# Batch 0's rows of the last expert picked by matmuls from SBUF, its other rows gathered while that expert runs

## The reference, cut to what matters

```python
probs = softmax(xr @ Wg); gate_vals, expert_idx = top_k(probs, 2)
# every row has a slot in each of its two experts; an expert holds C = 640 rows, later rows are dropped
dispatched = xr[dispatch_mask.reshape(-1) % S].reshape(E, C, d)       # 8 x 640 x 256
h = relu(einsum('ecd,edf->ecf', dispatched, w1))                      # 256 -> 1024
expert_out = einsum('ecf,efd->ecd', h, w2)                            # 1024 -> 256
out = gate_0 * (row of the first choice) + gate_1 * (row of the second choice)
```

## Time and profile before

| | us |
|---|---|
| median of three runs | 990.11 |
| the profiled execution | 992.42 |
| its span (first to last instruction) | 990.7 |
| PE busy | 916.7 (93%) |
| DVE busy | 605.8 (61%) |
| ACT busy | 492.0 (50%) |
| POOL busy | 439.3 (44%) |

### The profile page before, as it was taken

One profiled execution on the slowest core, in us unless ns is written; L12 is line 12 of the kernel. 1 busy time (PEld: TensorE's weight loads), 2 busy tenths in 40 slices (PEclk: granted clock), 3 DMA queues, 4 the chain that ended last, 5 costly groups with the idle time before them and its releaser, 6 DMA issues. The chain is left out here.

```text
span 990.7 us, 16978 instructions
## 1 busy us (share of the span) xinstructions
PE 916.7 (93%) x5620; PEld 718.8 (73%) x5620; DVE 605.8 (61%) x1961; ACT 492.0 (50%) x887; POOL 439.3 (44%) x416
## 2 busy tenths in 40 slices
PE   6899999999899999999992889999999779999997
PEld 4566766765688999999982556576756468888886
DVE  5677798988763444444444687887786246363535
ACT  6366666665333344443336265767676344343332
POOL 4453444436742333232236455455263455535333
PEclk9799999999999999999995898999999699999999
DMA  5443222201225322323104663534320010212201
GB/s 186 159 177 112 97 75 97 75 20 41 102 99 190 136 86 96 138 103 130 69 21 139 222 223 96 177 113 159 123 75 23 1 54 1 97 45 74 81 39 42
DMA packets 51964, 98.88 MB, mean 100 GB/s; under 512 B 7579, under 2 KB 23835, under 8 KB 51766
## 3 DMA queue, kind: packets, MB, share of 16 engines
q1 hardware_dynamic: 48822, 89.62, 26.3%
q0 software_dynamic: 3072, 8.39, 2.7%
HBM read 61.63 MB, written 36.36 MB: 99 GB/s over the span
## 5 line engine op out<-in xcount | busy, mean ns | idle before, releaser
L906 ACT ACTIVATE a_probs<-a_ps_b 128x512 f32<-128x512 f32 x240 | 142.0, 602 | 65.3 <-PE a_ps_b L985 62.4
L540 POOL TENSOR_SCALAR_AFFINE_SELECT a_probs<-a_probs 128x512 f32<-128x512 f32 x128 | 80.8, 649 | 136.2 <-ACT a_probs L906 136.1
L2074 PE MATMUL exp_ps_o<-w_both,exp_h_hi 128*128 128x512 f32 x320 | 115.7, 402 | 0.7 <-POOL w_both L1960 0.7
L985 PE MATMUL a_ps_b<-a_q_st,a_k_st 104*128 104x256 f32 (+3 forms) x384 | 104.7, 335 | 2.9 <-ACT a_probs L906 2.1
L1987 ACT ACTIVATE exp_h_hi<-shared 128x320 fp32r<-128x320 f32 x128 | 54.3, 440 | 86.0 <-PE shared L2057 86.0
L1274 DVE CUSTOM_DVE_ANT_0 a_masked_s<-shared,a_mask_f 128x512 f32<-128x512 f32 (+1 forms) x128 | 76.6, 620 | 31.8 <-PE shared L966 29.5
L2220 POOL TENSOR_TENSOR dense_h_lo<-dense_mixed,dense_h_hi 128x512 fp32r<-128x512 f32 x40 | 53.2, 1330 | 96.6 <-ACT dense_h_hi L2285 96.6
L1274 DVE CUSTOM_DVE_ANT_0 a_masked_s<-a_ps_a,a_mask_f 128x512 f32<-128x512 f32 (+1 forms) x128 | 76.5, 621 | 31.6 <-PE a_ps_a L966 29.0
L966 PE MATMUL a_ps_a<-a_k_st,a_q_st 96*128 96x512 f32 (+1 forms) x192 | 89.7, 483 | 5.8 <-DVE a_nmax L1274 5.0
L2031 DVE SCALAR_TENSOR_TENSOR exp_h_lo<-shared,exp_h_hi 128x320 fp32r<-128x320 f32 x128 | 61.4, 490 | 54.6 <-ACT exp_h_hi L1987 53.8
L966 PE MATMUL shared<-a_k_st,a_q_st 96*128 96x512 f32 (+1 forms) x176 | 90.0, 519 | 3.1 <-DMA a_k_st<-scratch 3.1
(11 more groups left out here) (326 smaller groups left out, 2244.8 us busy)
## 6 DMA issues: line engine op xcount, KB each, us to landing
w_raw<-in_m_w SPq DMA_DIRECT2D x16, 1024.0 KB, 5.4
scratch<-a_hi SPq DMA_DIRECT2D x24, 512.0 KB, 3.0
dense_mix_rows<-mix_rows SPq DMA_DIRECT2D x9, 768.0 KB, 6.4
scratch<-a_lo SPq DMA_DIRECT2D x24, 256.0 KB, 3.2
a_q_st<-scratch SPq DMA_DIRECT2D x64, 96.0 KB, 2.2
a_k_st<-scratch SPq DMA_DIRECT2D x64, 96.0 KB, 2.3
exp_rows<-dispatched SPq DMA_DIRECT2D x9, 640.0 KB, 3.9
dispatched<-kept_sub SPq DMA_DIRECT2D x9, 512.0 KB, 2.8
```

The source lines that it names most:

```text
L540: nc.gpsimd.affine_select(out=blocks, in_=blocks, compare_op=ALU.is_ge, fill=0.0, base=0, pattern=[[0, HPG], [1, P]], channel_multiplier=- ...
L906: nc.scalar.activation(probs[:, k, :], ps_b[k % B_BANKS][:, :], ACT.Exp, scale=scale).then_inc(exps, 1)
L985: last = nc.tensor.matmul(ps[:, at:at + wd], k_st[t % STACKS][0:TAIL, h, j * P:(j + 1) * P], q_st[t % STACKS][0:TAIL, h // PER_TILE, j * P ...
L2074: nc.tensor.matmul(bank[:, :], h[0][:, f, rows_at], w2["both"][:, f, :, :].rearrange("p k d -> p (k d)"), start=(f == 0), stop=False, skip ...
```

## The change

Three things, in the words of the code:

- **Expert 7's rows of batch 0 are selected on chip.** DVE writes `last_slots` (for each row of batch 0 the greater of its two slots) and `last_gate` (the weight with which the row uses expert 7, or 0) after batch 0's routing. SP writes the slots to a small DRAM tensor and, in the expert phase, reads them back to all partitions (`slot_rows`). In the second expert of every turn of the expert loop DVE writes five one-hot matrices `slot_hot` (128x512 each), one after every third half block; those of the last turn are used. When expert 7's output tiles are in `out`, ACT splits off the high part of each (`last_hi`), POOL the low part of the first four and DVE that of the last one, and PE multiplies: 5 tiles x 4 tiles of rows x 2 parts = 40 matmuls of 256 columns, placed after the loop, into the shared PSUM banks. DVE adds the result times `last_gate` to `sub`.
- **The other rows of batch 0 are gathered inside expert 7.** POOL's loop is cut to three turns and its last turn written out, without the split of a further w1. After the last w2 split POOL waits until expert 6 is stored and issues the eight gathers of batch 0 into `sub`. ACT and DVE weigh and add them. The rows of `results` that belong to expert 7 are zeroed beforehand by two more clearing transfers in attention 0. In attention 1 batch 0 begins with the statistics; POOL issues one gather of tile 4 ahead of the first root and three gathers (tile 4's other and tile 5's two) between the roots. ACT clears the second and third key stack later, after the first projections; DVE's `small_constants` stands after the first variance. SP stores expert 7's rows only once the gathers have landed.
- **PE's order at the end of attention 0.** `first_of_chip(2, 0)` and `(2, 1)` stand behind the projection of batch 3, `(2, 2)` behind its router transposes; `(2, 3)` stays at the end. Of the `keep_busy` ahead of `rt` one is left of three, ahead of `lg` none, and at the start of the expert phase one of two.

```diff
@@ attention_phase, SP @@
-                if rope and T < 6:
-                    clear_slots(3 * T, 3 * T + 3)
+                if rope and T < 7:
+                    clear_slots(3 * T, min(3 * T + 3, 2 * (E0 + 2)))
...
+                sp.wait_ge(first["slots_in"], 1)
+                sp.dma_start(first["list"], first["slots"][:, :]).then_inc(first["slots_out"], 16)
@@ attention_phase, POOL (layer 1) @@
-                for n in range(TPB + 1):
-                    gather(n)
+                gather(TPB, (0,))
                 combine_root(0, 0)
+                gather(TPB, (1,))
                 gather(TPB + 1)
                 combine_root(1, 0)
@@ attention_phase, ACT (layer 1) @@
                 clear_values(2 * TPB + 1)
-                for i in range(1, STACKS):
-                    clear_stack(i)
...
                 for j in ORDER[2:4]:
                     upper_evac(0, j)
+                for i in range(1, STACKS):
+                    clear_stack(i)
@@ attention_phase, PE (layer 0) @@
-            FINAL_TURNS = {("ot", BATCH - 1, 0): 1, ("rk", 2, 0): 1, ("rt", BATCH - 1, 0): 3, ("lg", BATCH - 1, 0): 1}
+            FINAL_TURNS = {("ot", BATCH - 1, 0): 1, ("rk", 2, 0): 1, ("rt", BATCH - 1, 0): 1}
...
                     first_of_memory()
-                    first_of_chip(2, 0)
                 fill_whole(name)
+                if rope and name == ("out", BATCH - 1, 1):
+                    for i in range(2):
+                        first_of_chip(2, i)
+                if rope and name == ("rt", BATCH - 1, 1):
+                    first_of_chip(2, 2)
             if rope:
-                for i in range(1, TPB):
-                    first_of_chip(2, i)
+                first_of_chip(2, TPB - 1)
@@ attention_phase, DVE @@
+            def last_expert_of_first():
+                at = slice(0, TPB)
+                nc.vector.tensor_tensor(first["slots"][:, :], slot[:, 0, at], slot[:, 1, at], ALU.max).then_inc(first["slots_in"], 1)
+                for k in range(2):
+                    last = nc.vector.scalar_tensor_tensor(last_gate[:, k, :], slot[:, k, at], float((E0 - 1) * CAP),
+                                                          gates[:, k, at], ALU.is_ge, ALU.mult)
+                after(last)
+                after(nc.vector.tensor_tensor(first["gate"][:, :], last_gate[:, 0, :], last_gate[:, 1, :], ALU.add))
...
-                small_constants()
-                for i in range(TPB):
-                    combine_sum(0, i)
-                combine_variance(0, 0)
+                for i in range(TPB):
+                    nc.vector.bn_stats(c_stats[:, i, :], tile(sub, i)).then_inc(c_stats_done[0], 1)
+                combine_variance(0, 0)
+                dve.sem_inc(scaled_done, TPB)
+                dve.sem_inc(summed, TPB)
+                small_constants()
...
+                    if rope and (T, s) == (16, 3):
+                        last_expert_of_first()
@@ expert_phase, SP @@
             load_weights(sp, "w1", w1, w1_in, 1)
+            sp.wait_ge(first["slots_out"], 16)
+            sp.dma_start(slot_rows[:, :], first["list"].rearrange("p n -> (p n)").unsqueeze(0).to_broadcast([P, SEQ]))\
+              .then_inc(slot_rows_in, 16)
...
             store(sp, E0 // PAIR - 1, 0)
+            sp.wait_ge(near_rows, 16 * 2 * TPB)
@@ expert_phase, POOL @@
-            with pool.Fori(0, E0 // PAIR) as it:
+            with pool.Fori(0, E0 // PAIR - 1) as it:
...
+            lower(w2, w2_hi_ready, E0 - 1, w2_ready)
+            lower(w1, w1_hi_ready, E0 - 1, w1_ready)
+            lower(w2, w2_hi_ready, E0, w2_ready)
+            pool.wait_ge(stored[0], 16 * (E0 // PAIR + 1))
+            pool.wait_ge(stored[1], 16 * (E0 // PAIR))
+            pool.wait_ge(first["scattered"], 16 * 2 * TILES)
+            for n in range(TPB):
+                for k in range(2):
+                    nc.gpsimd.indirect_dma_start(
+                        out=sub[:, k * TPB + n, :], out_offset=None, in_=results[:, :],
+                        in_offset=bass.IndirectOffsetOnAxis(ap=get_at[:, k, n:n + 1], axis=0),
+                        bounds_check=SLOTS - 1, oob_is_err=False).then_inc(near_rows, 16)
+            for t in range(CT - 1):
+                pool.wait_ge(last_hi, t + 1)
+                nc.gpsimd.tensor_tensor(last_part(1, t), out[PAIR - 1][:, t * D:(t + 1) * D], last_part(0, t).bitcast(F32),
+                                        ALU.subtract).then_inc(last_lo, 1)
@@ expert_phase, ACT, after its loop @@
+            act.wait_ge(t_free, E0 * T_FILLS + T_FILLS + T_BANKS)
+            for t in range(CT):
+                act.wait_ge(o_free, (E0 - 1) * O_FILLS + t + 1 + O_BANKS)
+                nc.scalar.copy(last_part(0, t), out[PAIR - 1][:, t * D:(t + 1) * D]).then_inc(last_hi, 1)
+                if t == 0:
+                    act.wait_ge(near_rows, 16 * 2 * TPB)
+                    for n in range(TPB):
+                        nc.scalar.activation(sub[:, n, :], sub[:, n, :], ACT.Identity, scale=gates[:, 0, n:n + 1])\
+                            .then_inc(near_scaled, 1)
@@ expert_phase, DVE @@
+                        if p == 1 and n % 3 == 0 and n // 3 < CT:
...
+                            nc.vector.tensor_scalar(slot_hot[:, n // 3, :].rearrange("q (i p) -> q i p", i=TPB),
+                                                    slot_rows[:, :].rearrange("q (p i) -> q i p", i=TPB), slot_ids[:, n // 3:n // 3 + 1], None,
+                                                    ALU.is_equal).then_inc(hots_done, 1)
...
+            dve.wait_ge(last_hi, CT)
+            nc.vector.tensor_tensor(last_part(1, CT - 1), out[PAIR - 1][:, (CT - 1) * D:CT * D],
+                                    last_part(0, CT - 1).bitcast(F32), ALU.subtract).then_inc(end_lo, 1)
+            for n in range(TPB):
+                dve.wait_ge(near_scaled, n + 1)
+                nc.vector.scalar_tensor_tensor(sub[:, n, :], sub[:, TPB + n, :], gates[:, 1, n:n + 1], sub[:, n, :], ALU.mult,
+                                               ALU.add).then_inc(near_sums, 1)
+            dve.wait_ge(near_sums, TPB)
+            for n in range(TPB):
+                dve.wait_ge(picked_full, n + 1)
+                nc.vector.scalar_tensor_tensor(sub[:, n, :], picked(n), first["gate"][:, n:n + 1], sub[:, n, :], ALU.mult,
+                                               ALU.add).then_inc(near_done, 1)
@@ expert_phase, PE @@
-            keep_busy(nc, ps_o[0], ident, keep["x"][:, 0:2, :].rearrange("p a d -> p (a d)"), 2)
+            keep_busy(nc, ps_o[0], ident, keep["x"][:, 0:2, :].rearrange("p a d -> p (a d)"), 1)
... after the loop
+            pe.wait_ge(u_free, E0 * U_FILLS + U_BANKS)
+            pe.wait_ge(hots_done, CT * (E0 // PAIR))
+            for t in range(CT):
+                pe.wait_ge(last_hi, t + 1)
+                if t < CT - 1:
+                    pe.wait_ge(last_lo, t + 1)
+                else:
+                    pe.wait_ge(end_lo, 1)
+                for i in range(TPB):
+                    for k in range(2):
+                        last = nc.tensor.matmul(picked(i), slot_hot[:, t, i * P:(i + 1) * P], last_part(k, t),
+                                                start=(t == 0 and k == 0), stop=(t == CT - 1 and k == 1),
+                                                skip_group_check=True)
+                    if t == CT - 1:
+                        last.then_inc(picked_full, 1)
```

More of the change, by code:

```diff
@@ L484, in clear_slots @@
                     e, at = divmod(m, 2)
-                    slots = w["dispatched"][e * CAP:(e + 1) * CAP, :].rearrange("(p t) d -> p t d", t=CT)
+                    rows = w["dispatched"][e * CAP:(e + 1) * CAP, :] if e <= E0 else w["results"][(E0 - 1) * CAP:E0 * CAP, :]
+                    slots = rows.rearrange("(p t) d -> p t d", t=CT)
                     a, n = at * CLEAR, min(CLEAR, CT - at * CLEAR)
@@ L530, in normalise @@
                 if b == BATCH - 1 and i == 0 and rope:
-                    pool.wait_ge(keep["cleared"], 16 * (E0 + 1) * -(-CT // CLEAR))
+                    pool.wait_ge(keep["cleared"], 16 * (E0 + 2) * -(-CT // CLEAR))
                 nc.gpsimd.tensor_scalar(tile(sub, n), tile(x, n), mean[:, n:n + 1],
@@ L621, in rows_lower, with gather @@
                                         ALU.subtract).then_inc(rows_lo, 1)
-            def gather(n):
+            def gather(n, choices=(0, 1)):
                 if n >= DEEP:
                     pool.wait_ge(summed, n - DEEP + 1)
-                for k in range(2):
+                for k in choices:
                     nc.gpsimd.indirect_dma_start(
@@ L1113, in first_of_memory @@
                                                  w1["rows"][:, t, c * P:(c + 1) * P], ident[:, a - t * P:z - t * P],
-                                                 start=(a == half * HALF), stop=False, skip_group_check=True)
+                                                 start=False, stop=False, skip_group_check=True)
```

(24 more changed lines are left out.)

13 lines of the change are left out of this document (9 added, 4 removed).

## The result

The changed kernel takes 1005.66 us (median of 4 runs, 1004.17 to 1007.25); the kernel before, run beside it, 990.23 (4 runs). The ratio is 1.0167, 95% interval 1.0144 to 1.0191. The prediction was 982.4 us: the time moved the other way. The profiled execution after took 1004.17 us (span 1002.4), 11.75 more than that of before (992.42, span 990.7).

A forecast was written before the change was run, and what follows sets the result against it. It took the end of the experts to be set by the chain from last output tile through store and gathers to batch 0's rows; 3.9 - 12.7 + 0.4 - 1.0 + 1.7 = -7.7 against 990.11 gave 982.4 us, range 978.8 to 986.5.

The forecast's parts named there:

- 1c: Inside the experts: expert 7's gathers are hidden and the five selections of each odd expert fit DVE's idle time; cost 0.
- The rival on the slower side: Odd experts' hidden layers: DVE becomes the bound, and from about 1.85 us a selection the gain is lost; chance 0.05.
- The rival of strided reads: Odd experts: each selection takes 1.1 us, twice 0.55, through its step of four; +1.4 us, 983.8; chance 0.15.
- 1a: Tail of the experts: 40 selection products take 5.0 us, then DVE's additions, so layer 1 starts later; +3.9 us.
- 1b: Head of layer 1: batch 0's gathers, waits and sums go, rows come earlier; -12.7 us, net -8.8 with 1a.
- Selection bound by weight loads: Tail of the experts: the 40 products take 7.3 us in place of 5.0; +2.3 us, 984.7; chance 0.10.
- the +0.4: Head of layer 1: PE's turns, waiting for weights, end after the rows; shorter transposes give half back; +0.4 us.
- Late gathers in expert 7: POOL let go only at 512 instead of 502, so rows land at 525; +3.5 us, 985.9; chance 0.05.
- Part 2: End of attention 0: with PE's new order the rank products come earlier and PE ends at 278.7; -1.0 us.
- the clock: Start of the experts: PE stands still longer, its clock falls, 3.4 us at half speed; +1.7 us, bounds 0 and 3.4.

The follow-up runs named there:

- two_turns_again: Rerun on the third chip of `two_turns`, beside `all_moved_again`: two turns in place of one at the experts' start; 975.37 us, ratio 0.9854.
- all_moved: The changed kernel with the five selections of odd experts behind half blocks 0, 2, 4, 5 and 13, none where POOL splits w2; 979.71 us, ratio 0.9894.
- two_turns: `all_moved` with two turns in place of one at the experts' start, on a slower chip; 997.27 us, ratio 0.9945.
- old_order: `all_moved` with PE's old order at the end of attention 0 and both turns at the experts' start, on a slower chip; 997.49 us, ratio 0.9943.
- old_order_again: Rerun of `old_order` on the third chip, beside `all_moved_again`; 979.22 us, ratio 0.9891.
- probe_reduce: The kernel before with one DVE tensor_reduce on SBUF added behind half block 6 of each odd expert, third chip; 987.75 us, ratio 0.9973.
- all_moved_again: Rerun of `all_moved`, the same kernel, on the third chip; 979.94 us, ratio 0.9893.
- third_moved: The changed kernel with only the third selection of odd experts moved, from behind half block 6 to behind 5; 984.75 us, ratio 0.9949.
- narrow: The changed kernel with only 32 of the third selection's 512 values behind half block 6, the other 480 behind 13; 999.56 us, ratio 1.0082.
- contiguous: The changed kernel with selections reading and writing in plain order, without the step of four (another result, same work); 1004.01 us, ratio 1.0121.
- probe_scalar: The kernel before with one contiguous 512-value DVE tensor_scalar on SBUF added behind half block 6 of odd experts, slower chip; 1024.5 us, ratio 1.0217.

## Why the prediction was wrong, step by step

**1c, the selections: the step that failed.** It counted DVE's idle time, 0.39 in each half block and 1.17 in three, and put the cost at 0. The rate was near: 0.68 each against 0.55 assumed, well inside 1.17. What it left out is that the third lands in POOL's split of w2 and is held until the end of it. That costs 3.8 us of PE's waiting and 2.7 more that go with the half clock behind it, 6.5 an odd expert, 26 in all. The rival on the slower side, with a chance of 0.05, named the right engine, experts and wait, but as a rate of 1.85 us or more a piece; no selection but the held one is slower than 0.7, and one instruction does it all. The rival of strided reads is refuted too: a step of four gives 0.68, not 1.1, and no loss (the experts take 234.5 us in `two_turns_again`, with the strided selections, and 234.6 before).

The trace of before did show it, in rows that I didn't read. First DVE, then POOL, in the kernel before, in layer 1's attention:

```profile
591.21 1.29 DVE L1510 SCALAR_TENSOR_TENSOR kept_x<-kept_sub,a_c_inv,kept_x 128x256 f32<-128x256 f32 x1
592.42 0.54 DVE L1274 CUSTOM_DVE_ANT_0 a_masked_s<-a_ps_a,a_mask_f 128x384 f32<-128x384 f32 x1
...
592.89 1.29 DVE L1510 SCALAR_TENSOR_TENSOR kept_x<-kept_sub,a_c_inv,kept_x 128x256 f32<-128x256 f32 x1
```
```profile
590.67 1.54 POOL L707 TENSOR_TENSOR w_gate_lo<-a_wide_raw,w_gate_hi 128x640 fp32r<-128x640 f32 x1
592.18 1.73 POOL L707 TENSOR_TENSOR w_up_lo<-a_wide_raw,w_up_hi 128x640 fp32r<-128x640 f32 x1
```

Line 1510 has two inputs in SBUF. Its median is 0.48; here it takes 1.29 twice, ending 0.29 and 0.27 after POOL's instruction each time (592.21, 593.91). Between them L1274, which reads PSUM, lies beside the same POOL work and takes 0.54, its usual length. The evacuations of the earlier trace rows run beside w2's split at their usual 0.49, and `shared`, one of their two inputs, lies in PSUM. They were the wrong rows to take for an instruction that reads and writes SBUF only. The POOL row at 592.18 is 0.16 longer than the median of its line and tile (1.57), and POOL's next instruction (L540, at 593.87) takes 0.82 where the line's median is 0.64; each begins while DVE's held one ends. That would fit POOL being held in turn, but two rows don't show it.

**1a, 1b, the boundary: right, but not its last step.** 4.7 us for the 40 products (5.0 predicted, the lower bound 4.7). Counted from the end of the last output product, as the prediction does, the statistics come after 6.1 us (6.8 predicted) and the rows after 14.55 (15.2). Counted from its start, as in the table, the rows come after 14.80 to 14.84 in the six traces of `all_moved`, `two_turns` and `old_order`, before after 24.24. Selection bound by weight loads is refuted. That PE next waits for the weights is right, and for that reason the rows no longer end the hole alone. In the kernel after the transposes start 0.47 after the rows, as before, and take the same 1.46, so the +0.4 charged there did not come; but that is luck, since the 22 turns took 4.09 us in place of 4.88. In `all_moved` the turns take 4.67, the transposes start 0.95 after the rows and take 1.04, much as forecast. In `old_order_again`, where the weights come later, they start 2.25 after them.

```profile
528.36 4.96 PE L45 MATMUL a_ps_b<-kept_ident 128*128 128x128 f32 x22 [7.29 <-DMA a_w_o<-in_a_o]
533.11 1.20 PE L1148 MATMUL a_ps_m<-kept_ident,kept_sub 128*128 128x128 f32 x8
```

Late gathers in expert 7 (0.05) did not show after: they are issued from 521.44, just behind the split, and hidden. ACT's four clears of the key stacks (573.30 to 580.96) are over 1.83 before batch 1's rows come: hidden too.

**Layer 1: undecided in size.** +0.4 was predicted, -4.7 seen. Before's profiled execution has its clock at half for 17 us from 774.8, after's for 3.4 near there. `probe_reduce`, whose layer 1 is that of before, needs 442.6 from its rows to the end; the three changed kernels on its chip need 442.3, 444.5 and 445.7. So the 4.7 can't be put down to the change.

**Part 2 and the clock: the fall right, the gain too large.** The first product comes 1.45 earlier (1.0 predicted), which is luck. The projection of batch 3, behind which the new order begins, already starts 1.09 earlier. Before, then after:

```profile
253.83 3.69 PE L1080 MATMUL a_ps_m<-early_o,a_o_t 128*128 128x256 f32 x16 [0.45 <-DVE a_picked L1408]
283.92 0.41 PE L2057 MATMUL shared<-exp_x_t_hi,w_hi 128*128 128x320 f32 x1 [0.30 <-DVEq L2024]
```
```profile
252.74 3.69 PE L1083 MATMUL a_ps_m<-early_o,a_o_t 128*128 128x256 f32 x16 [0.45 <-DVE a_picked L1414]
282.47 0.63 PE L2140 MATMUL shared<-exp_x_t_hi,w_hi 128*128 128x320 f32 x1 [1.16 <-DVEq L2088]
```

From the projection to the first product it is 30.09 before and 29.73 after: the order gives 0.4, not 1.0. Where the 1.09 come from no run shows; in the other profiles, those of the slower chip left aside, the projection starts between 250.03 and 253.81, under either order. The clock stood at half from 282.2 to 285.7, 3.4 us, as forecast. Its price there: POOL's first split in the experts starts 11.66 after the first product in place of 10.20, so 1.5 (1.7 predicted). That `two_turns_again` gives 1.8 is no second reading of it, since the fall in `all_moved_again` lasts 6.8. Nor is the fall certain: `third_moved`, with one turn, has none there.

With the selections moved the rest of the sum comes near: 1.06 and 1.07% are 10.5 us on 990, where -7.7 had been predicted; of the 2.8 missing 0.6 lies in the boundary, and the rest can't be placed, since layer 1 alone varies by more. The range, 978.8 to 986.5, holds the 979.7 and 979.9 of the kernel with the selections moved; nothing in it allowed for the hold.

## What to carry to other kernels

An idle share is not room: before an instruction is put into an engine's idle time, find which instruction of the other engine lies beside it and whether the two can run together. Take the price from a row with the same kind of operation and the same memories, and look in the trace for the longest length of such a line, not its mean. A long POOL operation near a DVE operation from SBUF to SBUF is a place to avoid; in these runs an operation with one of its inputs in PSUM and a reduction passed.

## What the runs showed of the hardware

- A DVE `tensor_scalar` or two-input operation on SBUF that starts during POOL's `tensor_tensor` on SBUF waits for the end of it, whatever its own size (32 values: 4.00 us), and then ends 0.05 to 0.49 us after it. A reduction of 512 values in the same place takes 0.70.
- A step of four float32 costs a 512-value `tensor_scalar` 0.68 us in place of 0.48.
- Behind a wait of 3.8 us PE had 6.8 us at half clock, four times out of four; behind 3.4 to 3.6 us (`narrow`, `contiguous`, `probe_scalar`) sometimes 3.4 and sometimes 6.8; behind 1.2 us (`third_moved`) none.
- The same kernel, with two turns, takes 975.37 us on one chip and 997.27 on another. Of the 23.2 us between their profiles 12.5 arise before the experts, 4.4 in them and 6.3 in layer 1. In expert 7, beside the gathers, one ACT instruction starts 3.4 us after its input is there on the slower chip (first row; input at 521.09) and PE then waits; on the other it starts at once (second row; input at 506.92). The kernel has a gather every 1.30 us there on both. What holds ACT the trace doesn't show, and it was not settled.

```profile
524.49 0.86 ACT L2028 CAST exp_x_t_hi<-exp_ps_t 128x512 fp32r<-128x512 f32 x2 [4.23 <-PE exp_ps_t L2131]
```
```profile
506.96 0.59 ACT L2028 CAST exp_x_t_hi<-exp_ps_t 128x512 fp32r<-128x512 f32 x1 [0.87 <-PE exp_ps_t L2131]
```
